# The shift by the maxima issued ahead of the weighted sums on TensorE

## The chip, the cores and the metric

The kernel runs on one core of a Trainium2 chip. What is measured is the device time of one launch in microseconds. The five engines of the core each work through a queue of their own: TensorE (PE, with its weight loads shown apart as PEld), VectorE (DVE), ScalarE (ACT), GpSimd (POOL) and SyncE (SP), which issues the transfers. They are tied together by semaphores alone: an instruction that waits holds everything behind it on its own engine.

## The reference, cut to what matters

Multi-head self-attention over 2048 small items of 40 fields each, four heads of width 32, with a linear residual and a ReLU:

```python
# x: (2048, 40, 64); Wq, Wk, Wv, Wr: (128, 64)
q = (x @ Wq.T + bq).reshape(B, F, 4, 32)
k = (x @ Wk.T + bk).reshape(B, F, 4, 32)
v = (x @ Wv.T + bv).reshape(B, F, 4, 32)
att = softmax(einsum('bfhd,bghd->bhfg', q, k) / 8, axis=-1)
out = einsum('bhfg,bghd->bfhd', att, v).reshape(B, F, 128)
return relu(out + x @ Wr.T + br)
```

The softmax is taken with maxima subtracted from the scores before the exponential. Any shift that is the same for all keys of a query leaves the softmax as it is.

## The kernel before

One step handles `GROUP` = 8 items, so there are 256 steps, written out one after the other. Each engine has a `group(n, place)` that is called for n = 0 to 255 and issues its share of several steps at once, in a pipeline. What step n's group issues, engine by engine and in this order:

- PE: `queries_and_keys(n)` (lines 386 and 390), `scores(n-1)` (406), `attend(n-3)` (475, the weighted sums of the values and of a column of ones), `shift(n-2)` (452), `values_and_residual(n)` (433, 438, 422).
- DVE: `max_of_keys(n-2)` (331, 332, 336), `keys(n)` (320), `max_of_quadrants(n-1)` (325), `normalise(n-3)` (341, a reciprocal), `divide(n-3)` (347).
- POOL: `diagonals(n-2)` (183), `query_columns(n)` (199, two instructions), `add_residual(n-4)` (191).
- ACT: `queries(n)` (231), `values_and_residual(n-1)` (258), `swap_maxima(n-1)` (244), `exponentials(n-2)` (251), `relu(n-5)` (238).
- SP: the loads of step n+8 and the stores of step n-5.

The maxima of step m travel like this: DVE takes maxima of the scores (325), ACT swaps halves (244), DVE joins them and splits the result into two bf16 parts (331, 332, 336), POOL spreads these into a diagonal `m_diag` of negative numbers (183), and PE multiplies this diagonal with `pick` and adds it onto the scores where they lie in PSUM (`shift`, 452). ACT then takes the exponential into `pT` (251), and one group later PE forms the weighted sums from `pT` and `rv` (`attend`, 475) into `o_bank`.

`o_bank` has two users in turn. In `queries_and_keys` it takes the queries and keys, in `attend` the weighted sums. So `queries_and_keys(n)` waits until `divide` of four steps back has read the sums (`att_ready`), and `attend(n-3)` waits until ACT and DVE have copied out the queries and keys of step n (`copied`). `shift` waits for POOL's diagonal (`diag_ready`), and `diagonals` for both halves of `m_split` (`m_ready`) and for the shift before it (`shifted`), since `m_diag` has one buffer. The exponentials wait for `shifted`, and for the weighted sums of two steps back, since `pT` has two buffers. SP waits for `o_made` (set by `attend`) before it loads the second half of x eight steps ahead and for `shifted` before the second store.

The order on each engine is the order of the calls in `group`; no scheduler moves anything. After step 255 a loop over three more groups drains the pipeline.

Of the kernel before, what the change touches and what calls it, by code (L numbers as in the profile page):

```python
# [34 lines left out]
def attention_kernel(nc, xT_in, w_in, bias_in, vr_bias_in, const_in, out):  # L35
# [3 lines left out]
    with ExitStack() as ctx:  # L39
# [82 lines left out]
        def before(n, limit):  # L122
            return n < limit

        def exists(n):
            return 0 <= n < STEPS
# [245 lines left out]
        def _(pe):  # L372
# [5 lines left out]
            def queries_and_keys(n, place):  # L378
                if n == 0:
                    pe.wait_ge(x_loaded[0], 32)  # L380
                elif before(n, LAG + 1):
                    pe.wait_ge(copied, 2 * n)
                else:

                    pe.wait_ge(att_ready, n - LAG)
                nc.tensor.matmul(o_bank[:, 0, 0:TOK], w_cols[0:HALF, 0], tokens(place, 0), start=True, stop=True)  # L386
                if n > 0:

                    pe.wait_ge(q_ready, 2 * n)
                nc.tensor.matmul(o_bank[:, 1, 0:TOK], w_cols[HALF:P, 0], tokens(place, HALF),  # L390
                                 start=True, stop=True).then_inc(qk_made, 1)

            def scores(n, place):


                if not before(n, 2):
                    pe.wait_ge(p_ready, n - 1)
                if not exists(n + 1):
                    pe.wait_ge(q_ready, 2 * (n + 1))
                for slot in range(SLOTS):  # L400
                    for member in range(MEMBERS):
                        b = MEMBERS * slot + member
                        k = ORDER.index(b)
                        for t in range(2):
                            rows = slice(HALF * t, HALF * (t + 1))
                            mm = nc.tensor.matmul(s_buf[place % 2][HALF * member:HALF * member + FIELDS, t,  # L406
                                                                   2 * FIELDS * slot:2 * FIELDS * (slot + 1)],
                                                  kT[rows, place % 4, FIELDS * k:FIELDS * (k + 1)],
                                                  q_bd[rows, place % 4, b].rearrange("d s f -> d (s f)"),
                                                  start=(slot == 0), stop=False, skip_group_check=True)  # L410
                mm.then_inc(scores_made, 1)
# [35 lines left out]
            def shift(n, place):  # L447
                pe.wait_ge(diag_ready, n + 1)
                for t in range(2):
                    for member in range(MEMBERS):  # L450
                        rows = slice(HALF * member, HALF * (member + 1))
                        mm = nc.tensor.matmul(s_buf[place % 2][HALF * member:HALF * member + FIELDS, t, 0:TOK],  # L452
                                              pick[rows, member, 0:FIELDS],
                                              m_diag[rows, t * (BLOCKS // 2):(t + 1) * (BLOCKS // 2)].rearrange("k b i -> k (b i)"),
                                              start=False, stop=True, skip_group_check=True)
                mm.then_inc(shifted, 1)

            def attend(n, place):


                if exists(n + LAG):
                    pe.wait_ge(copied, 2 * (n + LAG + 1))
                else:
                    pe.wait_ge(att_ready, n)
                if not exists(n + 2):
                    pe.wait_ge(p_ready, n + 1)
                if not exists(n + 1):
                    pe.wait_ge(vr_ready, n + 1)
                for idx in range(2):
                    for h in range(HEADS):  # L470
                        for c, slot in ((0, CROSSED + idx), (1, idx)):
                            for member in range(MEMBERS):
                                g = member ^ c
                                at = (2 * slot + h % 2) * FIELDS
                                mm = nc.tensor.matmul(o_part[HALF * g:HALF * g + FIELDS, c, idx * HEADS + h],  # L475
                                                      pT[HALF * member:HALF * (member + 1), place % 2, h // 2, at:at + FIELDS],
                                                      rv[HALF * member:HALF * (member + 1), place % 4, VALUES[slot] * HEADS + h],
                                                      start=True, stop=True, skip_group_check=True)
                mm.then_inc(o_made, 1)
# [3 lines left out]
            def group(n, place):  # L483
                queries_and_keys(n, place)
                if not before(n, 1):
                    scores(n - 1, place + 7)
                if not before(n, 3):
                    attend(n - 3, place + 5)
                if not before(n, 2):
                    shift(n - 2, place + 6)  # L490
                values_and_residual(n, place)

            run(group)
            for n in range(STEPS, STEPS + 3):
                if exists(n - 1):
                    scores(n - 1, n - 1)
                attend(n - 3, n - 3)
                if exists(n - 2):
                    shift(n - 2, n - 2)


_INS = ["r_x", "L0_rec_Wq", "L0_rec_bq", "L0_rec_Wk", "L0_rec_bk", "L0_rec_Wv", "L0_rec_bv", "L0_rec_Wr", "L0_rec_br"]
# [45 lines left out]
```

## Time and profile before

| what | value |
|---|---|
| median of 3 runs | 927.33 us (925.72 to 928.43) |
| profiled execution | 923.84 us |
| span of its instructions | 921.1 us |
| granted TensorE clock, mean | 0.996 |
| PE busy | 892.3 us (97%) |
| POOL busy | 872.1 us (95%) |
| ACT busy | 770.6 us (84%) |
| DVE busy | 726.7 us (79%) |
| all DMA queues | 101.20 MB, mean 110 GB/s |

The profiled execution took 923.84 us, of which 921.1 us lie between its first and its last instruction. Two engines are busy almost all the time, but the busy time of PE counts matmuls from start to modelled end, and they overlap, so that 97% is no proof that PE lacks time. In a timeline a row gives the start, the length, the engine, the line and the tile; rows of one line that follow each other closely are merged, with their number behind an x. What follows in brackets is the idle time of the engine just before and what ended it.

### The profile page before, as it was taken

To read this page: it belongs to the slowest core of one execution; us is meant where nothing else is said; L and a number is where in the kernel's file an instruction comes from. 1 tells how busy PE (TensorE), PEld (TensorE's weight loads), DVE (VectorE), ACT (ScalarE), POOL (GpSimd) and SP (SyncE) were. 2 spreads that over 40 slices of the span, in tenths; PEclk is the share of its full clock that TensorE was granted. 3 is DMA by queue.
4 is the path that set the end of the run, shared out by engine and by line. 5 is a ranking of instruction groups with operands and counts; after the bars stand their busy time and mean duration, and the time that the engine had idled before them with its cause. 6 is when DMAs were issued, how large, how long until landed. Compare 5 with 4: busy or idle time off the path is not lost.

```text
span 921.1 us, 67888 instructions
## 1 busy us (share of the span) xinstructions
PE 892.3 (97%) x30208; PEld 626.7 (68%) x30208; DVE 726.7 (79%) x2066; ACT 770.6 (84%) x1541; POOL 872.1 (95%) x1028
## 2 busy tenths in 40 slices
PE   6999999999999999999999999999999999999996
PEld 4667666767666776676666667666667766767664
DVE  5878777878787877888887878787878887878785
ACT  4888888888888888888888888888888888888886
POOL 3999999999999999999999999999999999999997
PEclk9999999999999999999999999999999999999998
DMA  4333333333333333333333333333333333333321
GB/s 120 97 110 117 113 105 110 115 107 112 118 112 107 116 111 111 111 117 109 115 112 105 110 111 111 112 112 112 117 111 112 112 120 108 115 110 112 111 83 67
DMA packets 67429, 101.20 MB, mean 110 GB/s; under 512 B 13632, under 2 KB 46656, under 8 KB 67136
## 3 DMA queue, kind: packets, MB, share of 16 engines
q1 hardware_dynamic: 66704, 96.72, 34.7%
q8 instruction: 235, 3.85, 1.8%
q14 instruction: 58, 0.48, 0.2%
q10 hardware_dynamic: 432, 0.15, 0.1%
HBM read 54.88 MB, written 41.94 MB: 105 GB/s over the span
## 4 chain that ended last, share of the span: by engine, by line
PE 93%; POOL 3%; issue 2%; DVE 1%; DMA 0%; ACT 0%; POOLq 0%; ACTq 0%
PE vr_bank L422 24%; PE o_bank L475 22%; PE s_buf L406 19%; PE o_bank L386 15%; PE s_buf L452 7%; PE vr_bank L433 6%; POOL y_sum L191 1%; POOL m_diag L183 1%; POOL q_bd L199 1%; PE o_bank L390 0%; DMA biases<-bias_in 0%; ACT y_rows L238 0%; POOLq L39 0%; DVE s_buf L325 0%; PE vr_bank L438 0%
## 5 line engine op out<-in xcount | busy, mean ns | idle before, releaser
L183 POOL TENSOR_TENSOR m_diag<-m_split,ident 128x640 bf16<-128x640 bf16 x256 | 323.1, 1262 | 32.2 <-DVE m_split L336 30.1
L191 POOL TENSOR_TENSOR y_sum<-rv,y_att 128x512 f32<-128x512 f32 x256 | 303.9, 1187 | 1.9 <-DVE y_att L347 1.9
L199 POOL TENSOR_SCALAR q_bd<-q_flat,consts 128x320 f32<-128x320 f32 x512 | 267.6, 537 | 11.2 <-DVE kT L320 11.1
L422 PE MATMUL vr_bank<-w_cols,xT 64*128 64x128 f32 (+1 forms) x3072 | 269.0, 308 | 0.1
L258 ACT ACTIVATE rv<-vr_bank 128x1024 f32<-128x1024 f32 x256 | 260.4, 1017 | 0.1
L325 DVE TRANSPOSE_TENSOR_REDUCE s_buf<-s_buf 128x20 f32<-128x640 f32 x256 | 221.6, 866 | 47.8 <-PE s_buf L406 47.7
L475 PE MATMUL o_bank<-rv,pT 64*40 64x33 f32 x16384 | 229.6, 202 | 12.1 <-issue 8.4
L406 PEld LDWEIGHTS s_buf<-q_bd,kT 64*40 64x40 f32 x8192 | 151.5, 113 | 116.2 <-issue 115.1
L475 PEld LDWEIGHTS o_bank<-rv,pT 64*40 64x40 f32 x16384 | 192.9, 117 | 54.4 <-issue 17.9
L320 DVE TENSOR_SCALAR kT<-o_bank,biases 128x320 f32<-128x320 f32 x256 | 140.9, 550 | 89.1 <-PE o_bank L390 89.0
L406 PE MATMUL s_buf<-q_bd,kT 64*40 64x80 f32 x8192 | 200.5, 233 | 1.4 <-issue 1.1
L422 PEld LDWEIGHTS vr_bank<-w_cols,xT 64*128 64x128 f32 x3072 | 195.2, 190 | 0.2 <-issue 0.2
L231 ACT ACTIVATE q_flat<-o_bank,biases 128x320 f32<-128x320 f32 x256 | 135.1, 528 | 71.5 <-PE o_bank L390 66.9
L386 PE MATMUL o_bank<-xT,w_cols 64*128 64x320 f32 x512 | 186.8, 445 | 5.7 <-DMA xT<-xT_in 5.7
L251 ACT ACTIVATE pT<-s_buf 128x640 f32<-128x640 f32 x256 | 180.4, 705 | 14.1 <-PE s_buf L452 8.0
L390 PE MATMUL o_bank<-xT,w_cols 64*128 64x320 f32 x512 | 187.5, 446 | 0.0
L347 DVE TENSOR_TENSOR y_att<-o_bank,r_sum 128x512 f32<-128x512 f32 x256 | 177.0, 691 | 9.2 <-DVE r_sum L341 0.3
L238 ACT ACTIVATE y_rows<-y_sum 128x512 f32<-128x512 f32 x256 | 159.1, 622 | 2.5 <-POOL y_sum L191 2.4
L244 ACT COPY m_swap<-s_buf 32x20 f32<-32x20 f32 x512 | 85.9, 168 | 55.5 <-DVE s_buf L325 49.4
L452 PE MATMUL s_buf<-m_diag,pick 64*40 64x320 bf16 x1024 | 114.9, 297 | 2.0 <-POOL m_diag L183 1.6
L386 PEld LDWEIGHTS o_bank<-xT,w_cols 64*128 64x128 f32 x512 | 76.6, 186 | 45.7 <-DVE y_att L347 35.4
L336 DVE TENSOR_TENSOR m_split<-s_buf,m_split 32x20 bf16<-32x20 f32 x512 | 88.5, 173 | 16.6
(31 smaller groups left out, 466.0 us busy)
## 6 DMA issues: line engine op xcount, KB each, us to landing
xT<-xT_in SPq DMA_DIRECT2D x512, 104.0 KB, 2.7
y<-y_rows SPq DMA_DIRECT2D x512, 80.0 KB
w_cols<-w_in SPq DMA_DIRECT2D x1, 192.0 KB, 2.6
vr_bias<-vr_bias_in ACTq DMA_DIRECT2D x1, 128.0 KB, 3.3
consts<-consts_in ACTq DMA_DIRECT2D x1, 20.0 KB, 2.4
biases<-bias_in ACTq DMA_DIRECT2D x1, 1.0 KB, 3.8
```

The lines of the kernel that those rows point to most:

```text
L183: pool.tensor_tensor(m_diag[:], m_split[:, place % 2].unsqueeze(2).to_broadcast([P, BLOCKS, QUAD]), ident[:].unsqueeze(1).to_broadcast([P, ...
L191: pool.tensor_tensor(y_sum[:, n % 3].rearrange("r (a d) -> r a d", d=DIM), rv[:, place % 4, RESIDUAL * HEADS:(RESIDUAL + SLOTS) * HEADS, 0 ...
L199: pool.tensor_scalar(q_bd[:, place % 4, :, s], q_flat[:, place % 2].rearrange("d (b f) -> d b f", f=FIELDS), consts[:, C_HEAD + s:C_HEAD + ...
L251: nc.scalar.activation(pT[:, place % 2], s_buf[place % 2][:, :, 0:TOK], ACT.Exp, scale=SCALE).then_inc(p_ready, 1)
L258: nc.scalar.activation(rv[:, place % 4, :, 0:DIM], vr_bank[:].rearrange("k t (a d) -> k (t a) d", d=DIM), ACT.Copy).then_inc(vr_ready, 1)
L325: nc.vector.tensor_reduce(m_part[place % 2].rearrange("k (t b) -> k t b", t=2), s_buf[place % 2][:, :, 0:TOK].rearrange("k t (b c) -> k t ...
L386: nc.tensor.matmul(o_bank[:, 0, 0:TOK], w_cols[0:HALF, 0], tokens(place, 0), start=True, stop=True)
L390: nc.tensor.matmul(o_bank[:, 1, 0:TOK], w_cols[HALF:P, 0], tokens(place, HALF), start=True, stop=True).then_inc(qk_made, 1)
L406: mm = nc.tensor.matmul(s_buf[place % 2][HALF * member:HALF * member + FIELDS, t, 2 * FIELDS * slot:2 * FIELDS * (slot + 1)], kT[rows, pla ...
L422: return nc.tensor.matmul(blocks(half, first, step)[:, 0:count], xT[rows, place % 8, PAIR * pair:PAIR * pair + P], w_cols[rows, 1:1 + coun ...
L452: mm = nc.tensor.matmul(s_buf[place % 2][HALF * member:HALF * member + FIELDS, t, 0:TOK], pick[rows, member, 0:FIELDS], m_diag[rows, t * ( ...
L475: mm = nc.tensor.matmul(o_part[HALF * g:HALF * g + FIELDS, c, idx * HEADS + h], pT[HALF * member:HALF * (member + 1), place % 2, h // 2, a ...
```

## The change

In PE's `group` the call of `shift(n-2)` is moved to stand between `scores(n-1)` and `attend(n-3)`; before, it stood behind `attend(n-3)`. The same is done in the draining loop. No instruction is added, removed or altered, and no semaphore's value.

```diff
                 if not before(n, 1):
                     scores(n - 1, place + 7)
+                if not before(n, 2):
+                    shift(n - 2, place + 6)
                 if not before(n, 3):
                     attend(n - 3, place + 5)
-                if not before(n, 2):
-                    shift(n - 2, place + 6)
                 values_and_residual(n, place)
...
                 if exists(n - 1):
                     scores(n - 1, n - 1)
-                attend(n - 3, n - 3)
                 if exists(n - 2):
                     shift(n - 2, n - 2)
+                attend(n - 3, n - 3)
```

PE's queue in the steady part, one group from its queries to the next group's scores, before (L475 is `attend`, L452 `shift`; x15 means fifteen more of the same):

```order
598 L386 MATMUL o_bank<-xT,w_cols 128x320 [waits att_ready]
599 L390 MATMUL o_bank<-xT,w_cols 128x320 [waits q_ready]
600 L406 MATMUL s_buf0<-q_bd,kT 40x80 [waits p_ready]
601 L406 MATMUL s_buf0<-q_bd,kT 40x80 x15
602 L475 MATMUL o_bank<-rv,pT 40x33 [waits copied]
603 L475 MATMUL o_bank<-rv,pT 40x33 x31
604 L452 MATMUL s_buf1<-m_diag,pick 40x320 [waits diag_ready]
605 L452 MATMUL s_buf1<-m_diag,pick 40x320 x3
606 L433 MATMUL vr_bank<-bias_rows,bias_pick 128x2x128 [waits vr_ready]
```

The same place of PE's queue with the change:

```order
600 L406 MATMUL s_buf0<-q_bd,kT 40x80 [waits p_ready]
601 L406 MATMUL s_buf0<-q_bd,kT 40x80 x15
602 L452 MATMUL s_buf1<-m_diag,pick 40x320 [waits diag_ready]
603 L452 MATMUL s_buf1<-m_diag,pick 40x320 x3
604 L475 MATMUL o_bank<-rv,pT 40x33 [waits copied]
605 L475 MATMUL o_bank<-rv,pT 40x33 x31
606 L433 MATMUL vr_bank<-bias_rows,bias_pick 128x2x128 [waits vr_ready]
```

The four matmuls of L452 and their wait for the diagonal have moved ahead of the 32 of L475.

The end of PE's queue, in the draining loop, before:

```order
3317 L475 MATMUL o_bank<-rv,pT 40x33 [waits att_ready]
3318 L475 MATMUL o_bank<-rv,pT 40x33 x31
3319 L452 MATMUL s_buf0<-m_diag,pick 40x320 [waits diag_ready]
3320 L452 MATMUL s_buf0<-m_diag,pick 40x320 x3
3321 L475 MATMUL o_bank<-rv,pT 40x33 [waits p_ready,att_ready]
3322 L475 MATMUL o_bank<-rv,pT 40x33 x31
3323 L452 MATMUL s_buf1<-m_diag,pick 40x320 [waits diag_ready]
3324 L452 MATMUL s_buf1<-m_diag,pick 40x320 x3
3325 L475 MATMUL o_bank<-rv,pT 40x33 [waits vr_ready,p_ready,att_ready]
```

and with the change:

```order
3317 L452 MATMUL s_buf0<-m_diag,pick 40x320 [waits diag_ready]
3318 L452 MATMUL s_buf0<-m_diag,pick 40x320 x3
3319 L475 MATMUL o_bank<-rv,pT 40x33 [waits att_ready]
3320 L475 MATMUL o_bank<-rv,pT 40x33 x31
3321 L452 MATMUL s_buf1<-m_diag,pick 40x320 [waits diag_ready]
3322 L452 MATMUL s_buf1<-m_diag,pick 40x320 x3
3323 L475 MATMUL o_bank<-rv,pT 40x33 [waits p_ready,att_ready]
3324 L475 MATMUL o_bank<-rv,pT 40x33 x31
3325 L475 MATMUL o_bank<-rv,pT 40x33 [waits vr_ready,p_ready,att_ready]
```

Each shift has moved ahead of one group of weighted sums, so that the last two groups of sums now stand next to each other. The queues of DVE, ACT, POOL and SP are word for word the same.

## Rows read from the trace of the kernel before

**Rows 1.** The page: busy shares, and the chain that ended last, by engine.

```profile
PE 892.3 (97%) x30208; PEld 626.7 (68%) x30208; DVE 726.7 (79%) x2066; ACT 770.6 (84%) x1541; POOL 872.1 (95%) x1028
...
PE 93%; POOL 3%; issue 2%; DVE 1%; DMA 0%; ACT 0%; POOLq 0%; ACTq 0%
```

**Rows 2.** Timeline of one undisturbed step, all engines (start, length, engine, line, tile).

```profile
22.64 0.82 PE L475 MATMUL o_bank<-rv,pT 64*40 64x33 f32 x64
...
23.27 0.44 PE L452 MATMUL s_buf<-m_diag,pick 64*40 64x320 bf16 x4
...
23.52 0.26 DVE L341 RECIPROCAL r_sum<-o_bank 128x16 f32<-128x16 f32 x1
...
23.65 0.28 PE L433 MATMUL vr_bank<-bias_rows,bias_pick 64*128 64x256 bf16 x1
...
24.43 0.18 DVE L331 TENSOR_TENSOR s_buf<-s_buf,m_swap 128x20 f32<-128x20 f32 x1
...
24.56 0.18 PEld L386 LDWEIGHTS o_bank<-xT,w_cols 64*128 64x128 f32 x1 [0.15 <-DVE y_att L347]
...
24.71 0.38 DVE L336 TENSOR_TENSOR m_split<-s_buf,m_split 32x20 bf16<-32x20 f32 x2
...
25.18 1.25 POOL L183 TENSOR_TENSOR m_diag<-m_split,ident 128x640 bf16<-128x640 bf16 x1
...
25.30 0.76 PE L406 MATMUL s_buf<-q_bd,kT 64*40 64x80 f32 x32
25.42 0.53 ACT L231 ACTIVATE q_flat<-o_bank,biases 128x320 f32<-128x320 f32 x1 [0.68 <-PE o_bank L390]
...
26.02 0.82 PE L475 MATMUL o_bank<-rv,pT 64*40 64x33 f32 x64
```

**Rows 3.** Timeline at the two places where PE waits for the diagonal.

```profile
15.20 1.26 POOL L183 TENSOR_TENSOR m_diag<-m_split,ident 128x640 bf16<-128x640 bf16 x1 [1.62 <-DVE m_split L336]
...
16.52 0.45 PE L452 MATMUL s_buf<-m_diag,pick 64*40 64x320 bf16 x4 [0.73 <-POOL m_diag L183]
...
16.90 0.28 PE L433 MATMUL vr_bank<-bias_rows,bias_pick 64*128 64x256 bf16 x1
...
911.12 1.26 POOL L183 TENSOR_TENSOR m_diag<-m_split,ident 128x640 bf16<-128x640 bf16 x1 [0.65 <-ACT y_rows L238]
...
912.43 0.45 PE L452 MATMUL s_buf<-m_diag,pick 64*40 64x320 bf16 x4 [0.88 <-POOL m_diag L183]
```

**Rows 4.** Timeline: reciprocals of the first and the last full group, and the drain's.

```profile
20.14 0.26 DVE L341 RECIPROCAL r_sum<-o_bank 128x16 f32<-128x16 f32 x1
...
906.42 0.26 DVE L341 RECIPROCAL r_sum<-o_bank 128x16 f32<-128x16 f32 x1
...
909.47 0.26 DVE L341 RECIPROCAL r_sum<-o_bank 128x16 f32<-128x16 f32 x1
...
911.60 0.26 DVE L341 RECIPROCAL r_sum<-o_bank 128x16 f32<-128x16 f32 x1 [0.56 <-PE o_bank L475]
...
915.49 0.26 DVE L341 RECIPROCAL r_sum<-o_bank 128x16 f32<-128x16 f32 x1 [2.90 <-PE o_bank L475]
```

**Rows 5.** Timeline of a step in which the weighted sums stand still.

```profile
502.03 0.49 PE L475 MATMUL o_bank<-rv,pT 64*40 64x33 f32 x26
...
502.84 0.54 PE L475 MATMUL o_bank<-rv,pT 64*40 64x33 f32 x36 [0.32 <-issue]
...
503.19 0.32 PE L452 MATMUL s_buf<-m_diag,pick 64*40 64x320 bf16 x2
...
503.32 0.32 PE L452 MATMUL s_buf<-m_diag,pick 64*40 64x320 bf16 x2
```

**Rows 6.** Timeline of the drain, weighted sums at its end.

```profile
914.58 0.87 PE L475 MATMUL o_bank<-rv,pT 64*40 64x33 f32 x35 [0.36 <-issue]
```

**Rows 7.** Granted clock (PEclk) by window: the drain's end, and before it.

```profile
core 0: us, PE busy (x) PEld busy (x) DVE busy (x) ACT busy (x) POOL busy (x), PEclk, DMA share, GB/s
913.00:916.00 3.00, 1.37 (x64) 1.15 (x64) 0.48 (x2) 2.29 (x4) 1.65 (x2) 0.75 0.24 81
880.00:905.00 25.00, 25.00 (x849) 17.46 (x851) 20.45 (x62) 22.16 (x45) 25.00 (x30) 1.00 0.21 67
```

## The prediction

> **What bounds the kernel now.** I read the page first. PE and POOL are both busy nearly all the time, and the chain that ended last runs over PE for 93% of the span [rows 1]. That says where to look, not what the limit is, so the next view is the timeline of one undisturbed step [rows 2]. There the weighted sums (L475) start at 22.64 and again at 26.02: a step of 3.38 us. Followed back, that step is a ring through three engines. From the start of the sums to the reciprocal that reads them (L341) it is 0.88 us (22.64 to 23.52). From there the divide (L347) runs, and the weight load of the next queries (L386), whose idle time ended with y_att, starts at 24.56: 1.04 us. The queries and keys take until the scores (L406) start at 25.30: 0.74 us. The scores take until the sums start at 26.02: 0.72 us. 0.88 + 1.04 + 0.74 + 0.72 = 3.38 us. (What the sums wait for by name, the copy of the queries, L231, ends at 25.95, so it is no later than the scores.) Call this the ring of the queries. The shift (L452, at 23.27) and the values and residual (L433 at 23.65, L422 behind it) do not lengthen it: they run while DVE divides.
>
> The real step is a little longer. Reciprocals of the first and the last full group stand at 20.14 and 906.42 with 252 steps between them [rows 4], which is 886.28 / 252 = 3.517 us a step. The difference, 0.137 us a step, is standstills inside the weighted sums in some of the steps: in one of them L475 stops for 0.32 us for nothing that the profile shows, after 26 of its matmuls [rows 5].
>
> A second path matters for the change. In the same step, the maxima of the next shift are joined by DVE directly behind the divide, in DVE's own order: L331 at 24.43, L336 from 24.71, 0.38 us long. POOL starts the diagonal (L183) at 25.18, which is 1.66 us behind the reciprocal [rows 2]. In this step the diagonal ends at 26.43 (25.18 + 1.25), while PE's shift comes only behind the sums, at 23.27 + 3.38 = 26.65. So the diagonal is finished before PE asks for it, and there is no wait.
>
> **The change, part by part.** No instruction is added or removed, so busy times stay. What changes is what PE waits for, and who waits for PE.
>
> *The shift now stands ahead of the sums, and PE reaches it before its diagonal is there.* PE gets to the shift where the sums used to start, 2.50 us behind the reciprocal (1.04 + 0.74 + 0.72). The diagonal starts 1.66 us behind it. How long after the start of a diagonal the shift can start is shown where PE does wait for it: 15.20 to 16.52 and 911.12 to 912.43, so 1.32 and 1.31 us [rows 3]. 1.66 + 1.32 = 2.98, so PE stands still for 0.48 us in each step. Behind the waiting shift are queued the weighted sums, and behind them the values and residual. DVE waits for the sums.
>
> *That closes a ring that was open.* The sums of step n-3 release the reciprocal and the divide. Behind these, in DVE's order, the maxima of step n-1 are joined. POOL spreads them, and the shift of n-1 now precedes the sums of n-2, in the next group. Before, that shift came behind the sums, and the ring took two groups. Its length now, term by term:
> - start of the sums to the reciprocal: 0.88 us [rows 2]
> - reciprocal to the start of the diagonal: 1.66 us [rows 2]
> - start of the diagonal to the start of the shift: 1.32 us [rows 3]
> - start of the shift to the start of the sums: not in the trace. The four matmuls start in two pairs 0.13 us apart (503.19 and 503.32) [rows 5]; two pairs then take about 0.27 us, the lower bound. The next work behind a shift, L433, starts 0.38 us after it, twice (23.27 to 23.65, 16.52 to 16.90) [rows 2, 3]; with 0.02 for rounding 0.40 is the upper bound. I take 0.30, near the lower one, since L433 changes the shape of the weights from 64*40 to 64*128 and L475 keeps 64*40, and since going from L475 to L452 shows no gap.
>
> The sum is 0.88 + 1.66 + 1.32 + 0.30 = 4.16 us.
>
> Those two gaps also agree with a rule. The Trainium skill, TensorEngine Tiling (Array Packing), section Tiling Modes, says that changing the tiling mode drains TensorE while changing only the tile does not. By that rule this term is the bare 0.27 us and the forecast 8 us lower; without it the 0.38 us of L433 would hold for the sums too and the forecast would be 20 us higher. No row of before has a shift directly ahead of sums.
>
> *Standstills.* They cost 0.137 us a step now, inside the sums, and the sums are on the new ring as well. In their favour PE now pauses 0.48 us ahead of the shift, with its queue free to fill. Bounds 0 and 0.137; I take 0.05.
>
> *What the other engines do.* The second store waits for an earlier shift, the second load of x for later sums; both are eight or four buffers deep, and a longer step gives them more time. POOL's work of a step fits in the undisturbed 3.38 us, and so in 4.21. ACT gets its shifted scores sooner, but the sums that use the exponentials come a group later, so nothing is gained there. The queries still wait for the divide, but are no longer on the longest ring. Between the end of the values and residual and the queries PE waits some more; that costs nothing.
>
> *Start and end.* The first sums now stand behind a diagonal, some 0.3 us. In the drain the last two groups of sums and their shifts are still in a line: the first two intervals of the drain's reciprocals, 3.05 and 2.13 us, grow to about 4.2 each, and the last one, 3.89 us, in which PE waited for a diagonal [rows 3, 4], shrinks by 1 to 2 us, since its shift now stands one place earlier. Together about +2 us.
>
> **The sum.** 4.16 + 0.05 = 4.21 us a step against 3.517: 0.693 x 252 = 174.6 us. With 2 us for both ends that is 923.84 + 176.6 = 1100.4 us for a profiled execution. The profiled one lies 3.5 us below the median of the runs shown, so 1104 us is forecast for the median. Low end: 0.27 and no standstills, 4.13 us a step, 1084 us. High end: 0.40 and 0.137, 4.397 us a step, 1151 us.
>
> **Rivals.**
>
> *The diagonal is in time, and only the shift's own stream is added.* If the diagonal came 0.48 us sooner, the ring of the queries would decide, with the shift now inside it: 3.38 + 0.30 + 0.06 = 3.74 us a step, +56 us and 2 for the ends, 985 us. For it speaks that DVE and POOL have idle time. Against it, that the joining of the maxima stands behind the divide in DVE's order and starts as soon as the divide lets it, so the delay moves along with the sums. Chance 0.06.
>
> *Not slower: the move is free and the standstills go.* PE's added pause would have to fall into time in which it stands still today; then the step falls to the 3.38 us of the ring, 252 x 0.137 = 35 us less, 893 us. It decides from the point where shift and wait lie in a gap, that is when the new ring is 3.52 us or shorter; it is 4.16, so 0.64 us would have to come out of a chain whose terms are all measured but one. Chance 0.02.
>
> *The clock falls.* PE would pause twice in each step, and the clock did fall while PE waited in the drain: 0.75 on average from 913 to 916 against 1.00 from 880 to 905 [rows 7]. The two levels are 2.4 and 1.2 GHz. At the lower one 35 matmuls of the sums took 0.87 us [rows 6], about 1.4 us for 64 against 0.82 [rows 2], so +0.55 a step, and the shift +0.27: 5.03 us a step, 1310 us. Against it: the steps before hold pauses too, at clock 1.00, and the drain's pauses were near 1 us. Chance 0.04. The Trainium skill, TensorE: Matmul & The Clock Gate, section A second HAM failure mode, describes such a kernel, in which short idle times between groups of matmuls made the clock swing; in the trace of before the clock stays at its upper level with standstills of 0.32 us, which speaks against it here.
>
> *The change does nothing* is excluded: the queue of PE differs in every group, and no other engine's queue does.
>
> **How the numbers follow.** Forecast 0.86, ring of the queries 0.06, clock 0.04, not slower 0.02, something else that slows 0.02. The range of 1078 to 1150 us is the forecast's own low and high end with a few us below for the rounding of four terms. Slower by over 0.3% (about what a measurement of this kernel can tell from no change) has 0.98; the "not slower" case is split evenly into 0.01 faster and 0.01 within 0.3%.
>
> **What would show it.** Reciprocals 4.1 to 4.3 us apart. PE waiting before L452 for POOL's diagonal in nearly every step, near 0.5 us, the largest wait on PE. Diagonals still starting 1.66 us behind the reciprocal. POOL's share of busy time down to about 80%. The step from L452 to L475 between 0.27 and 0.40 us. Wrong if the diagonal starts earlier against the reciprocal, if PE waits for something else, if the standstills grow, or if the clock drops.

## The result and the profile after

The changed kernel takes 1071.55 us (median of 4 runs, 1071.17 to 1072.21), against 926.53 us for the kernel before (922.76 to 928.43): a ratio of 1.157, 95% interval 1.153 to 1.161. The direction and the mechanism are as forecast; the time lies 6 us below the low end of the range of 1078 to 1150 us.

The page of the changed kernel, busy shares and the chain that ended last, beside [rows 1]:

```profile
PE 943.2 (88%) x30208; PEld 665.5 (62%) x30208; DVE 742.8 (69%) x2066; ACT 769.6 (72%) x1541; POOL 875.8 (82%) x1028
...
DVE 36%; POOL 31%; PE 27%; issue 6%; DMA 0%; ACT 0%; POOLq 0%; ACTq 0%
POOL m_diag L183 30%; PE o_bank L475 17%; DVE y_att L347 16%; PE s_buf L452 10%; DVE m_split L336 8%; DVE r_sum L341 6%; DVE s_buf L331 2%; DVE m_split L332 2%; POOL y_sum L191 0%; DMA biases<-bias_in 0%; PE vr_bank L422 0%; PE o_bank L386 0%; POOLq L39 0%; ACT rv L258 0%; DVE s_buf L325 0%
```

Before, 93% of the chain lay on PE. Now three engines share it, and its lines are those of the forecast ring, with all others at 0%: diagonal (L183), shift (L452), sums (L475), reciprocal (L341), divide (L347), joining of the maxima (L331 to L336). The work of POOL and ACT is what it was; their shares fall because the span grew. The queries and scores, a third of the chain before, are gone from it.

One step of the changed kernel, beside [rows 2]:

```profile
499.81 0.26 DVE L341 RECIPROCAL r_sum<-o_bank 128x16 f32<-128x16 f32 x1 [0.62 <-PE o_bank L475]
...
501.45 1.26 POOL L183 TENSOR_TENSOR m_diag<-m_split,ident 128x640 bf16<-128x640 bf16 x1 [0.68 <-DVE m_split L336]
...
502.77 0.31 PE L452 MATMUL s_buf<-m_diag,pick 64*40 64x320 bf16 x2 [0.41 <-POOL m_diag L183]
...
502.80 0.27 PE L475 MATMUL o_bank<-rv,pT 64*40 64x33 f32 x4
502.92 0.30 PE L452 MATMUL s_buf<-m_diag,pick 64*40 64x320 bf16 x2
503.05 0.79 PE L475 MATMUL o_bank<-rv,pT 64*40 64x33 f32 x60
...
503.91 0.26 DVE L341 RECIPROCAL r_sum<-o_bank 128x16 f32<-128x16 f32 x1 [0.62 <-PE o_bank L475]
```

Reciprocal to diagonal 1.64 us, diagonal to shift 1.32, shift to the next reciprocal 1.14: 4.10 us. The last reciprocal of a full group stands at 1052.88 and the first at 20.47, so the mean of 252 steps is 1032.41 / 252 = 4.097 us, and the median step is 4.10 as well: all steps are alike.

The waits, summed over the run (engine, line, releaser, us, times, longest):

```profile
POOL m_diag L183 <- DVE m_split L336: 176.5, 256, 1.8
DVE r_sum L341 <- PE o_bank L475: 163.1, 256, 3.3
PEld s_buf L452 <- POOL m_diag L183: 156.1, 256, 3.1
...
PE s_buf L452 <- POOL m_diag L183: 109.6, 256, 3.0
```

PE waits for the diagonal in every one of the 256 steps, its weight load 0.61 us on average, where 0.48 us was forecast. No wait inside the sums for "issue" is left in the list of the changed kernel. That is a gain that goes the other way: the standstills of [rows 5] have vanished.

### The profile page after: what moved, and what is told of

Read it like the earlier page. It is cut to its first block, busy times and chain, and to the rows that moved or that the text cites. A ratio compares the mean times of both kernels' runs of the same rounds, so it can differ in the third digit from the quotient of the medians.

```text
span 1069.8 us, 67888 instructions
## 1 busy us (share of the span) xinstructions
PE 943.2 (88%) x30208; PEld 665.5 (62%) x30208; DVE 742.8 (69%) x2066; ACT 769.6 (72%) x1541; POOL 875.8 (82%) x1028
## 3 DMA queue, kind: packets, MB, share of 16 engines
q8 instruction: 236, 3.87, 1.6%
## 4 chain that ended last, share of the span: by engine, by line
DVE 36%; POOL 31%; PE 27%; issue 6%; DMA 0%; ACT 0%; POOLq 0%; ACTq 0%
POOL m_diag L183 30%; PE o_bank L475 17%; DVE y_att L347 16%; PE s_buf L452 10%; DVE m_split L336 8%; DVE r_sum L341 6%; DVE s_buf L331 2%; DVE m_split L332 2%; POOL y_sum L191 0%; DMA biases<-bias_in 0%; PE vr_bank L422 0%; PE o_bank L386 0%; POOLq L39 0%; ACT rv L258 0%; DVE s_buf L325 0%
## 5 line engine op out<-in xcount | busy, mean ns | idle before, releaser
L183 POOL TENSOR_TENSOR m_diag<-m_split,ident 128x640 bf16<-128x640 bf16 x256 | 322.4, 1259 | 176.5 <-DVE m_split L336 176.5
L475 PE MATMUL o_bank<-rv,pT 64*40 64x33 f32 x16384 | 266.8, 202 | 1.1 <-DVE y_att L347 1.1
L325 DVE TRANSPOSE_TENSOR_REDUCE s_buf<-s_buf 128x20 f32<-128x640 f32 x256 | 221.5, 865 | 41.9 <-PE s_buf L406 41.9
L475 PEld LDWEIGHTS o_bank<-rv,pT 64*40 64x40 f32 x16384 | 233.3, 116 | 6.3 <-DVE y_att L347 1.3
L386 PE MATMUL o_bank<-xT,w_cols 64*128 64x320 f32 x512 | 206.3, 483 | 8.4 <-DMA xT<-xT_in 5.6
L452 PE MATMUL s_buf<-m_diag,pick 64*40 64x320 bf16 x1024 | 115.2, 303 | 109.6 <-POOL m_diag L183 109.6
L390 PE MATMUL o_bank<-xT,w_cols 64*128 64x320 f32 x512 | 206.3, 483 | 0.0
L406 PE MATMUL s_buf<-q_bd,kT 64*40 64x80 f32 x8192 | 196.1, 233 | 0.0
L347 DVE TENSOR_TENSOR y_att<-o_bank,r_sum 128x512 f32<-128x512 f32 x256 | 177.0, 691 | 9.2 <-DVE r_sum L341 0.3
L341 DVE RECIPROCAL r_sum<-o_bank 128x16 f32<-128x16 f32 x256 | 66.0, 258 | 163.1 <-PE o_bank L475 163.1
L452 PEld LDWEIGHTS s_buf<-m_diag,pick 64*40 64x40 bf16 x1024 | 30.1, 94 | 156.1 <-POOL m_diag L183 156.1
```

The costliest lines, as they stand in the source:

```text
L183: pool.tensor_tensor(m_diag[:], m_split[:, place % 2].unsqueeze(2).to_broadcast([P, BLOCKS, QUAD]), ident[:].unsqueeze(1).to_broadcast([P, ...
L325: nc.vector.tensor_reduce(m_part[place % 2].rearrange("k (t b) -> k t b", t=2), s_buf[place % 2][:, :, 0:TOK].rearrange("k t (b c) -> k t ...
L347: nc.vector.tensor_tensor(y_att[:, place % 2].rearrange("r (c a d) -> r c a d", c=2, d=DIM), o_part[:, :, :, 0:DIM], r_sum[:].unsqueeze(3) ...
```

## The experiments

Each is compared with the kernel before on the chip it ran on. Runs of the kernel before differ between chips and runs, 908 to 930 us over all of them, while the changed kernel and most of the variants repeat within 0.2%. The step is the mean over the same 252 intervals between reciprocals, taken from each trace. "Standstills" are distances of over 0.15 us between the starts of two successive matmuls of the same line, in the sums or the scores, counted from the first to the last reciprocal of a full group. The traces come from several chips, so small differences between steps of different runs should not be read.

| kernel | us | step, us | standstills |
|---|---|---|---|
| before | 926.53 | 3.517 | 89 |
| changed | 1071.55 | 4.097 | 0 |
| e1 wait without the move | 1034.07 | 3.949 | 13 |
| e2 half diagonal | 941.86 | 3.587 | 15 |
| e3 changed, more PE work | 1073.27 | 4.096 | 0 |
| e4 before, more PE work | 1027.43 | 3.926 | 0 |
| e5 changed, 64 instructions more | 1162.41 | 4.438 | 74 |
| e6 maxima ahead of the divide | 1124.51 | 4.313 | 0 |
| e7 shift in the middle of the sums | 993.65 | 3.790 | 0 |
| e8 before, bf16 sums | 878.53 | 3.344 | 0 |
| e9 before, a second wait | 915.05 | 3.477 | 49 |
| e10 changed, 32 instructions more | 1075.50 | 4.110 | 7 |
| e11 changed, bf16 sums | 979.38 | 3.741 | 0 |

### e1: the wait without the move

```diff
                 else:
                     pe.wait_ge(att_ready, n)
+                if exists(n + 1):
+                    pe.wait_ge(diag_ready, n + 2)
```

> The order of the kernel before, in which the weighted sums of n-3 also wait for the diagonal of n-2, as if the shift stood ahead of them; the shift itself stays behind them. Theory (the ring through the diagonal): 0.88 us from the sums to the reciprocal, 1.64 to the diagonal, 1.31 to its reader, so 3.83 to 3.86 us a step; against 3.517 that is +80 to +87 us, about 1007 us. The difference to the changed kernel, 4.10 us a step, is then the stream of the shift, about 0.26 us. The standstills inside the sums are gone, since PE pauses before them. Rival (the shift's own stream in PE's order costs, not the wait): within 1% of the kernel before, 927 us.

Measured: 1034.07 us, a ratio of 1.127 (1.120 to 1.134). The order is that of the kernel before, and yet three quarters of the slowdown are there (0.43 of 0.58 us a step). So it is the wait for the diagonal that costs, not first of all the stream of the shift. The step is longer than expected by 0.1 us. The timeline of e1 (L477 are the sums) shows where most of that lies:

```profile
499.52 1.26 POOL L183 TENSOR_TENSOR m_diag<-m_split,ident 128x640 bf16<-128x640 bf16 x1 [0.50 <-DVE m_split L336]
...
500.92 0.80 PE L477 MATMUL o_bank<-rv,pT 64*40 64x33 f32 x62 [0.50 <-POOL m_diag L183]
...
501.80 0.26 DVE L341 RECIPROCAL r_sum<-o_bank 128x16 f32<-128x16 f32 x1 [0.44 <-PE o_bank L477]
...
503.44 1.26 POOL L183 TENSOR_TENSOR m_diag<-m_split,ident 128x640 bf16<-128x640 bf16 x1 [0.49 <-DVE m_split L336]
```

The sums start 1.40 us after the start of the diagonal, where the shift started 1.32 us after it; the rest of the ring is 0.88 + 1.64 as expected. e9 tests where the 0.08 us come from. The standstills were expected to go, and 13 short ones, of 0.16 to 0.41 us, are left; e5 and e10 come back to them.

### e9: a second wait that never holds

```diff
                 else:
                     pe.wait_ge(att_ready, n)
+                if exists(n + 1):
+                    pe.wait_ge(diag_ready, n + 1)
```

> The kernel before, in which the weighted sums of n-3 also wait for the diagonal of n-3, which has long been there: a second wait that never holds. In e1 the sums started 1.40 us after the start of the diagonal and not 1.31 us after it. Theory (a second wait on an instruction costs by itself): the sums start 0.05 to 0.1 us later behind the scores in each step, +12 to +25 us. Rival (the 0.09 us belongs to waiting for POOL at this instruction, not to the second wait): no change, within 0.5%.

Measured: 915.05 against 912.67 us, a ratio of 1.002 (1.000 to 1.004). A second wait that has long been fulfilled costs next to nothing (2 us, where 12 to 25 us were expected), so the theory of this run fell. That leaves the 0.08 us of e1 to a wait that really holds. Its trace has 254 instructions more than that of the kernel before, about one for each step with the added wait, so the second wait is an instruction of its own ahead of the matmul; that the matmul is only taken up once this one has passed would explain the 0.08 us, but no run shows it.

### e2: half of the diagonal

```diff
-                pool.tensor_tensor(m_diag[:], m_split[:, place % 2]...
+                pool.tensor_tensor(m_diag[:, 0:BLOCKS // 2], m_split[:, place % 2, 0:BLOCKS // 2]...
...
+            pool.memset(m_diag[:], 0.0)
```

> The changed kernel, in which POOL builds only the first half of the diagonal; the second half stays zero, so half of the shift by the maxima is left out of the computation, while PE does all its matmuls. Theory: L183 falls from 1.26 to about 0.65 us, the ring through the diagonal from 4.10 to 3.49 us, and so the ring of the queries decides, 3.38 us and the stream of the shift inside it, 3.61 to 3.65 us a step: 1071.5 - 252 x 0.46 = 955 us (948 to 962), not below the kernel before. Rival (PE or POOL as a whole is the bound, in proportion to POOL's work): POOL's busy time falls by 156 us and the time with it, 916 us. Rival (the diagonal does not bound): 1071 us.

Measured: 941.86 us, a ratio of 1.027 (1.022 to 1.032) to the kernel before. The median step is 3.56 us, 0.54 us less than 4.10, and the diagonal is 0.54 us shorter (0.72 us in place of 1.26). So the ring through the diagonal still sets the step. It was expected at 3.49 us because half of the diagonal was taken at 0.65 us. The mean step is 3.587 us, since 15 standstills are back. The time is 26 us above the 916 us that would follow if POOL's busy time as a whole were the bound. The timeline of e2 (L407 are the scores, L453 the shift, L342 the reciprocal):

```profile
502.66 0.72 POOL L183 TENSOR_TENSOR m_diag<-m_split,ident 128x320 bf16<-128x320 bf16 x1 [0.48 <-DVE m_split L337]
...
502.79 0.76 PE L407 MATMUL s_buf<-q_bd,kT 64*40 64x80 f32 x32
...
503.44 0.31 PE L453 MATMUL s_buf<-m_diag,pick 64*40 64x320 bf16 x2
...
504.57 0.26 DVE L342 RECIPROCAL r_sum<-o_bank 128x16 f32<-128x16 f32 x1
```

The diagonal is done at 503.38, and the shift starts at 503.44. Over 220 steps the median from the end of the diagonal to the start of the shift is 0.054 us in e2 and 0.054 us in the changed kernel: in both the shift starts as soon as the diagonal lets it, and the pause in e2 is only too short to be noted as idle time. (The shift starts 0.11 us after the last matmul of the scores has started; in e6, where it has no need to wait for the diagonal, it is 0.05 us.) The ring of the queries is therefore shorter still in this order, by an estimate from these two figures 3.50 us. No run has the diagonal early enough to show that step, so whether this order would then be slower than the kernel before stays open.

### e3 and e4: more work for PE in either kernel

```diff
                 nc.tensor.matmul(o_bank[:, 0, 0:TOK], w_cols[0:HALF, 0], tokens(place, 0), start=True, stop=True)
+                nc.tensor.matmul(o_bank[:, 0, 0:TOK], w_cols[0:HALF, 0], tokens(place, 0), start=True, stop=True)
```

> The changed kernel with the queries' matmul issued twice into the same place (the result is the same). PE has some 0.27 us more to do in each step, between the divide and the scores. Theory: PE waits 0.27 us less for the diagonal and nothing else changes: 1071 us, within 0.5%, step 4.10 us. Rival (PE's work is on the path in the changed kernel too): +0.27 us a step, +68 us, 1140 us.

> The kernel before with the queries' matmul issued twice into the same place (the result is the same). The ring of the queries, 3.38 us, grows by 0.27 to 3.65 us a step. All standstills inside the sums of the kernel before stand at the same instruction modulo 256, so they look like the supply of instructions in blocks of 256. If it is a rate (a block can't be had faster than about every 3.7 us), 240 instructions in 3.65 us leave time enough and the standstills go almost entirely: 3.65 to 3.68 us a step, +34 to +41 us, 960 to 968 us. Rival (they come because PE never pauses, or from traffic at that place): they stay at 0.12 to 0.14 us a step, 3.78 us, about 993 us.

Measured: 1073.27 us for the changed kernel and 1027.43 us for the kernel before. The price of the added matmul was mis-sized. In e4 the timeline shows:

```profile
501.91 0.18 PEld L386 LDWEIGHTS o_bank<-xT,w_cols 64*128 64x128 f32 x1 [0.15 <-DVE y_att L347]
...
502.56 0.70 PE L387 MATMUL o_bank<-xT,w_cols 64*128 64x320 f32 x2
...
503.18 0.58 PEld L407 LDWEIGHTS s_buf<-q_bd,kT 64*40 64x40 f32 x32 [0.44 <-issue]
```

From the queries' first weight load to the scores it is 1.27 us where [rows 2] have 0.74: 0.53 us more, not 0.27. The repeated matmul is two passes of 0.27 us, and the keys' matmul, which runs beside the first, does not cover them. With 0.53 the ring of the queries is 3.38 + 0.53 = 3.91 us, and 3.926 was measured. In the changed kernel the same 0.53 us cost nothing: the step is 4.096 us as against 4.097. That is the plainest sign that PE's own work between the divide and the shift is off the path there. It moves the rest of the cover to 0.61 - 0.53 = 0.08 us.

The standstills are gone in e4 although PE still hardly pauses: 240 instructions in 3.93 us have taken the place of 236 in 3.52. That speaks for a rate and against "PE never pauses", but with a step that much longer the run does not say what rate.

### e5 and e10: more instructions, hardly more work

```diff
                 if not before(n, 2):
                     pe.wait_ge(p_ready, n - 1)
...
+                if n >= 2:
+                    for i in range(32):
+                        rows = slice(HALF * (i % 2), HALF * (i % 2 + 1))
+                        nc.tensor.matmul(s_buf[place % 2][HALF * (i // 2 % 2):HALF * (i // 2 % 2) + FIELDS, i % 2, 0:8],
+                                         pick[rows, 0, 0:FIELDS], pick[rows, 0, 0:8],
+                                         start=True, stop=True, skip_group_check=True)
```

In e10 the loop has 16 rounds in place of 32.

> The changed kernel with 32 tiny matmuls of 8 columns ahead of the scores, in PE's pause; the scores overwrite what they write. 64 instructions more make 300 on PE in a step. By PE's time: 32 matmuls in two row groups of some 17 to 25 ns each are 0.5 us or less a step, nearly all of it inside the 0.60 us for which PE waits for the diagonal: 4.10 to 4.2 us a step, 1071 to 1095 us, and no standstills. By a rate of supply (256 instructions about every 3.7 us): 300 instructions need 4.34 us, standstills come back, 4.34 to 4.45 us a step, 1132 to 1160 us.

> The changed kernel with 16 tiny matmuls of 8 columns ahead of the scores, half of the dose of e5, 268 instructions on PE in a step. Theory (supply of instructions, a block of 256 not faster than about every 3.8 us): 268 instructions need 3.97 us, less than the 4.10 us of the ring: no standstills to speak of, 1071 to 1080 us. Rival (each added instruction costs, in proportion to e5, 91 us for 32 matmuls): +45 us, 1117 us.

Measured: 1162.41 us with 32 and 1075.50 us with 16. The first 16 matmuls cost 4 us, the next 16 another 87 us. The timeline of e5 has both kinds of steps (L403 are the tiny matmuls, L481 the sums, L458 the shift):

```profile
504.10 0.43 PE L481 MATMUL o_bank<-rv,pT 64*40 64x33 f32 x25
506.19 0.23 PE L481 MATMUL o_bank<-rv,pT 64*40 64x33 f32 x2 [1.66 <-issue]
...
508.24 0.36 PE L403 MATMUL s_buf<-pick 64*40 64x8 bf16 x32
508.45 0.78 PE L412 MATMUL s_buf<-q_bd,kT 64*40 64x80 f32 x32
509.41 0.31 PE L458 MATMUL s_buf<-m_diag,pick 64*40 64x320 bf16 x2 [0.18 <-POOL m_diag L183]
```

At 509.41 PE still waits 0.18 us for the diagonal, so by PE's time the 32 matmuls fit; the median step is 4.10 us. But in some steps the sums stand still, here for 1.66 us, and the mean is 4.438. Counted through all matmuls of the trace from 0, every one of the 74 standstills of e5 comes ahead of a matmul whose number leaves 94 when divided by 128, and so do all 89 of the kernel before, all 15 of e2 and all 7 of e10. A matmul and its weight load are two instructions, so the standstills come at every 256th (remainder 188). In e1 and e9 the place drifts through the step; counted with the one instruction more that each step has there, all 13 and all 49 come at remainder 188 or 189 of 256. So it is the number of the instruction that matters, and not what it does. The page of the changed kernel gives the size of the blocks in which instructions are fetched (packets, MB, share):

```profile
q8 instruction: 236, 3.87, 1.6%
```

60416 matmuls and loads are 236 blocks of 256, and 3.87 MB are 16 KB a block. For a block e5 takes 4.438 x 256 / 300 = 3.79 us on average, and the kernel before 3.517 x 256 / 236 = 3.82 us. Two kernels whose steps differ by 0.9 us run at the same pace for a block: the supply of instructions to PE is what both are near to. The changed kernel takes 4.097 x 256 / 236 = 4.44 us a block and has no standstill; e10, with 268 instructions in 4.11 us, takes 3.93 us and has 7.

The transfers of this queue are in the traces too, one for each block, and they tie the standstills to the supply. In the kernel before, the matmul behind each of the 89 standstills starts 1.2 to 1.7 us after the latest block has landed, and behind each of the 74 of e5 as well. In the changed kernel PE comes to the same place of each block 2.6 us after the landing at the median, and never under 1.7 us after it. e1 does not fit: it takes 4.27 us a block (237 instructions in 3.949 us), and 12 of its 13 short standstills come 2.0 to 2.4 us after the latest block has landed. What they are stays open.

The Trainium skill, Runtime: NRT & Kernel Launch, section Instruction fetch mechanics, says that an engine's instructions are refilled in blocks of 16 KiB, 256 instructions, and that crossing a block is mostly hidden. The traces agree on the block. They do not agree that it is hidden in kernels that need a block in less than 3.9 us: e2, at 3.89 us a block, has 15 standstills, and the kernel before has 89.

### e6: the maxima ahead of the divide

```diff
-                if not before(n, 2):
-                    max_of_keys(n - 2, place + 6)
                 keys(n, place)
...
                 if not before(n, 3):
                     normalise(n - 3, place + 5)
+                if not before(n, 1):
+                    max_of_keys(n - 1, place + 7)
+                if not before(n, 3):
                     divide(n - 3, place + 5)
...
```

> The changed kernel, in which DVE joins the maxima of the next shift between the reciprocal and the divide instead of behind the divide. The ring through the diagonal shrinks by the divide, some 0.6 us, to about 3.5 us; the ring of the queries grows by the joining, 0.66 us: 1.11 + 1.04 + 0.66 + 0.74 + 0.75 + 0.03 = 4.33 us a step. Theory (the longest ring decides): 4.30 to 4.35 us, +50 to +64 us, 1122 to 1136 us. Rival (only the diagonal's ring matters): 3.5 to 3.6 us a step, some 930 us.

Measured: 1124.51 us, a ratio of 1.214 (1.209 to 1.220), a step of 4.313 us where 4.30 to 4.35 was expected. The diagonal now comes sooner, but the queries wait for a later divide, and the longest ring decides. The wait list of e6 turns round: PE waits for the divide and no longer for the diagonal.

```profile
PEld o_bank L387 <- DVE y_att L347: 301.4, 252, 1.2
...
PE o_bank L387 <- DVE y_att L347: 200.1, 252, 0.8
```

### e7: the shift in the middle of the sums

```diff
                 for idx in range(2):
+                    if idx == 1 and exists(n + 1):
+                        shift(n + 1, n + 1)
                     for h in range(HEADS):
...
-                if not before(n, 2):
-                    shift(n - 2, place + 6)
+                if n == 2:
+                    shift(0, 0)
                 values_and_residual(n, place)
...
```

> The kernel before with the shift put between the first and the second half of the weighted sums. Theory: the ring through the diagonal holds the shift's stream, 0.26, the second half of the sums until the reciprocal, about 0.57, then 1.64 and 1.31: 3.78 us a step, +66 us, 993 us (980 to 1005), between the two kernels, and no standstills. Rival (it matters only that the shift is not behind the sums): like the changed kernel, 1071 us. Rival (half of the sums is cover enough): 927 us.

Measured: 993.65 us, a ratio of 1.073 (1.069 to 1.077), a step of 3.790 us where 3.78 was expected. The half of the sums that stands ahead of the shift, about 0.3 us, leaves the ring, and the step is shorter by just that. So the cost is not a matter of the order as such, but of how much work lies behind the shift in the same ring.

### e8 and e11: a shorter piece in the ring, in either order

```diff
-        pT = sb("pT", [P, 2, 2, TOK])
-        rv = sb("rv", [P, 4, 2 * SLOTS * HEADS, VW])
+        pT = sb("pT", [P, 2, 2, TOK], BF16)
+        rv = sb("rv", [P, 4, 2 * SLOTS * HEADS, VW], BF16)
```

> The order of the kernel before, with pT and rv (probabilities, values and residual) in bf16 in place of f32, so the result is coarser. Each matmul of the sums is one pass in place of two: 172 instructions a step on PE in place of 236, and the sums take perhaps 0.5 us in place of 0.88. Theory: the ring of the queries falls to about 3.0 us, the supply of instructions has room, no standstills, and POOL's own work decides, 3.38 us a step (its three pieces follow each other without a pause in the undisturbed step): 252 x 0.13 less, about 892 us, or less where POOL's work on rv gets cheaper. Rival (the ring or the supply is not what bounds): 927 us.

> The version with pT and rv in bf16 (e8), in the order of the changed kernel, so the shift stands ahead of the sums. Theory (the ring through the diagonal): 1.64 + 1.31 from the reciprocal to the shift, 0.26 for its stream and about 0.42 from the sums to the reciprocal (in e8 the sums' 32 matmuls take 0.38 us): 3.63 us a step against 3.34, 878.5 + 252 x 0.29 = 952 us. Rival (with the sums so short POOL stays the bound in either order): 879 us.

Measured: e8 878.53 us, a ratio of 0.949 (0.945 to 0.952) to the kernel before: it beats both kernels, at the price of coarser probabilities, values and residual. e11 979.38 us. The order alone costs 0.397 us a step here, against 0.580 in f32. e11 was expected at 952 us; its timeline shows the term that was too small:

```profile
501.78 0.31 PE L452 MATMUL s_buf<-m_diag,pick 64*40 64x320 bf16 x2 [0.41 <-POOL m_diag L183]
...
502.56 0.26 DVE L341 RECIPROCAL r_sum<-o_bank 128x16 f32<-128x16 f32 x1 [0.26 <-PE o_bank L475]
```

From the shift to the reciprocal it is 0.78 us, not 0.68. I had taken 0.42 us for the sums from the 0.38 us that they take in e8, but there the reciprocal does not follow them. The same places in e8:

```profile
500.52 0.38 PE L475 MATMUL o_bank<-rv,pT 64*40 64x33 bf16 x32
...
500.63 0.86 DVE L325 TRANSPOSE_TENSOR_REDUCE s_buf<-s_buf 128x20 f32<-128x640 f32 x1 [0.16 <-PE s_buf L406]
...
501.40 0.22 DVE L341 RECIPROCAL r_sum<-o_bank 128x16 f32<-128x16 f32 x1
```

The sums are done near 500.90, and the reciprocal starts at 501.40, when DVE comes free from the maxima of the quadrants (L325). So in e8 a third ring is at work, scores, maxima of the quadrants, reciprocal, divide, queries; POOL goes without a pause through the same 3.34 us. The pieces of that ring add up to the step, 0.83 us from the scores to L325, 0.77 to the reciprocal, 1.00 to the queries and 0.74 to the scores, 3.34 us. POOL's work is as long, so which of the two sets 3.34 us was not told apart.

## Why the prediction was right or wrong, point by point

**What bounded the kernel before.** The ring of the queries was read rightly in its length, and e4 confirms it: work added to it costs its full size. Three things were missed. First, what I called standstills "for nothing that the profile shows" is the limit of the supply of instructions (e5, e10), and the kernel before runs at it: the median step is 3.39 us, the mean 3.517. Second, two pieces of the ring end at a wait other than the one I named. The 0.72 us ahead of the sums end with the copies of the queries and keys, as this line of the kernel before shows, a copy that ends at 25.97, 0.05 us ahead of the sums at 26.02:

```profile
25.42 0.55 DVE L320 TENSOR_SCALAR kT<-o_bank,biases 128x320 f32<-128x320 f32 x1 [0.33 <-PE o_bank L390]
```

The reciprocal in [rows 2] starts as L325 leaves DVE; it has no idle time noted in front of it. Both lie so close to the ends I named that the sum is the same. But the shift need not wait for the copies, so in the changed kernel PE reaches it sooner than the 2.50 us that I took, and waits 0.61 us in place of 0.48. Third, POOL's own work is as long as that ring: in the undisturbed steps its pieces follow each other without a pause, so the kernel before has two bounds at 3.39 us, and no run tells which of them is the longer.

**The ring that closes.** Right. PE waits for the diagonal in all 256 steps, diagonals start 1.64 us behind the reciprocal, POOL is busy 82% of the span, the reciprocals are 4.10 us apart, inside the 4.1 to 4.3 forecast. e1, e2, e7 and e11 each change one piece of the ring, and the step follows; e6 shortens it until the ring of the queries is the longer one.

**The size.** Forecast 4.21 us a step, measured 4.097. The 0.113 us are made of four terms, up to rounding: standstills 0.05 against 0; shift to reciprocal 1.18 (0.30 + 0.88) against 1.14; reciprocal to diagonal 1.66 against 1.64; diagonal to shift 1.32 against about 1.315. Times 252 that is 28.5 us. The other 3.5 us come from carrying the distance of the profiled execution to the median of the runs over to the changed kernel: there the profiled execution (1071.66 us) stands at the median. The scatter of the kernel before fits its standstills, which the changed kernel does not have; no run here ties the two together directly.

**The step of it that failed** is the size of terms in the sum, not the path. The two terms that no row of the kernel before could show were both too large: the standstills, put at 0.05 us, measured 0 (12.6 us over 252 steps), and the stream of the shift, put at 0.30 us, measured 0.26, the 1.14 us from shift to reciprocal less 0.88 (10 us). The low end of the range failed with them. It had the standstills at 0 but still made 4.13 us a step: the stream was bounded below by 0.27 us, 0.02 us came from the reciprocal-to-diagonal term, read from one step and rounded at two rows (0.01 us in a term is 2.5 us in the sum), and the 3.5 us of scatter lay on the low end as well. I said "a few us" for all of this, and it was 12. The standstills' true value, 0, I had only as an end of the range, though the reason for it (PE pauses and its queue can fill) was there. e3, e6 and e7 have none either; e1 shows that a pause alone does not ensure it.

**The sign for the stream** was badly chosen. The first four matmuls of the sums start 0.03 us after the shift and the other 60 start from 0.28 us after it, so the distance from L452 to L475, forecast at 0.27 to 0.40 us, cannot be read as one figure. The 0.26 us are the difference of two others.

**Start and end.** Right: the first reciprocal comes 0.33 us later, and from the last full group to the last reciprocal it is 11.31 us (1052.88 to 1064.19) against 9.07: together 2.6 us, where 2 was forecast. The parts are less good than the sum: the drain's intervals are 4.09, 4.82 and 2.40 us, where about 4.2, 4.2 and 1.9 to 2.9 were forecast, and the sums of the second one ran at the lower clock (granted 0.50 from 1059 to 1062).

**The rivals.** The ring of the queries was put at 3.74 us and 985 us, with 0.06 us in it that no run shows. e2, at 3.56 us and 942 us, shows that this ring is shorter than that. The error is in part the wait for the copies again, which the shift does not share. Its ground for being unlikely was right: the joining of the maxima moves along with the divide. The clock did not fall in the steady part: 1.00 from 20 to 1053 us, and 0.995 over the whole run against 0.996. The move was not free: the 0.64 us that would have had to come out of the ring did not.

**The drain of TensorE between shapes** (the Trainium skill, TensorEngine Tiling (Array Packing), section Tiling Modes). By that rule a change of the tiling mode drains TensorE and a change of the tile alone does not; the traces agree. The bare 0.27 us that it gave is nearer to the measured 0.26 than the 0.30 I took: behind a shift, sums of the same shape follow with no gap. In the changed kernel the change of shape comes after the sums: L433 starts 0.13 us after the last of the sums, which follow each other at about 0.01 us. There it lies beside the divide and costs nothing.

## What to carry to other kernels

In a pipeline written out by hand, follow the ring of waits that the new order closes, through every engine's own queue, and count how many steps it spans: a ring that took two steps and now takes one puts its whole length into every step, however little work is moved. Put the waiting piece behind all work that can do without it; each microsecond that stays behind it in the ring is paid in every step (e7). And where a term is multiplied by 252 steps, take it from many steps, because 0.01 us of rounding is already 0.3% of the time.

## What the runs showed of the hardware that was not expected

The supply of instructions to TensorE is a limit of its own, near 3.8 us for a block of 256 on this kernel: e5 (3.79 us) and the kernel before (3.82 us) both run at it, with 0.15 to 2.1 us between two matmuls, always at the same instruction of a block. Standstills thin out as a block is given more time: 15 at 3.89 us (e2), 7 at 3.93 us (e10), none at 4.11 us (e7) and above, but for the 13 short ones of e1. The pace is not the same everywhere: e9, on the chip where the kernel before took 913 us and not 927, needs 3.76 us for a block. How far it depends on the transfers that run beside it was not tried.

Matmuls of different lines do not start strictly in their program order. In the changed kernel four matmuls of the sums start at 502.80, ahead of the second pair of the shift at 502.92, though all four of the shift come first in the queue. The same is seen in 255 of the 256 steps. They may be those sums whose result goes to the other half of the rows, so that they use a part of the array that the shift leaves free: in the kernel the sums alternate between the two halves, and the weight load that is first in the queue, the one with the wait for `copied`, starts only at 502.92. The rows do not name the part, so this is argued and not shown. The Trainium skill, TensorE: Matmul & The Clock Gate, section Part 2: What happens when you issue a matmul, says that matmuls stay in program order and only weight loads are pulled ahead. By the starts in this trace that does not hold here. Whether it is a reason why the shift's stream costs 0.26 us and not more, no run shows.
